# A fused two-layer recurrent block: FFN pair 1 at the end of a round, decayed keys turned through memory, and three other moves

## What is computed

```python
xn = _layernorm(x)
s  = _L0_attn_ref(xn, ...)          # recurrent attention with a decay per channel and token
g  = _silu(_L0_ffn_ref(xn, ...))    # gated FFN 256 -> 1024, 2 of 4 kept by magnitude, -> 256
x  = x + s * g
xn = _layernorm(x)
s  = _L1_attn_ref(xn, ...)          # state space layer, 8 heads, states of 64
g  = _silu(_L1_ffn_ref(xn, ...))    # gated FFN
x  = x + s * g
```

## Time and profile before

| | us |
|---|---|
| median of 3 runs (lowest to highest) | 735.85 (734.74 to 736.4) |
| the profiled execution | 735.66 |
| its span | 733.9 |
| PE busy | 711.3 (97%) |
| DVE busy | 497.5 (68%) |
| ACT busy | 342.0 (47%) |
| POOL busy | 77.2 (11%) |
| mean granted TensorE clock, 1 is full | 0.995 |
| PE's share of the chain that ended last | 76% |

### The profile page before, as it was taken

How to read it: one execution, slowest core, us unless ns; L and a number is a source line. 1 busy time by engine, 2 the same in 40 slices (tenths; PEclk the granted TensorE clock), 3 DMA queues, 4 the chain that set the end, 5 groups by cost and what they waited for, 6 DMA issues and landing times.

```text
span 733.9 us, 17949 instructions
## 1 busy us (share of the span) xinstructions
PE 711.3 (97%) x6896; PEld 590.1 (80%) x6896; DVE 497.5 (68%) x1207; ACT 342.0 (47%) x678; POOL 77.2 (11%) x85
## 2 busy tenths in 40 slices
PE   5998999999999999999999999999999999999998
PEld 3777688877888688886888868888788878888686
DVE  4976599547895478955787558855689547895133
ACT  1411685226832468215762168522584236821690
POOL 6301011101011010100111001110101101011020
PEclk9989999999999999999999999999999999999999
DMA  7900351125400353013531145102540136301360
GB/s 238 404 23 29 102 88 32 15 73 144 75 2 15 88 146 59 2 28 104 117 59 16 30 138 95 32 15 69 142 80 3 15 87 145 59 2 26 119 116 16
DMA packets 122444, 55.93 MB, mean 76 GB/s; under 512 B 104384, under 2 KB 114176, under 8 KB 120832
## 3 DMA queue, kind: packets, MB, share of 16 engines
q1 hardware_dynamic: 122368, 54.76, 30.3%
HBM read 42.35 MB, written 12.40 MB: 75 GB/s over the span
## 4 chain that ended last, share of the span: by engine, by line
PE 76%; DVE 12%; issue 5%; DMA 2%; SPq 2%; ACT 2%; POOL 1%; DVEq 0%; ACTq 0%; POOLq 0%
PE psum L1486 58%; PE psum L1707 2%; PE psum L1722 2%; PE psum L1514 2%; PE psum L1565 1%; PE psum L1760 1%; PE psum L1931 1%; PE psum L1595 1%; PE psum L1733 1%; DVE beats L1085 1%; PE psum L1577 1%; DVE own L992 1%; PE psum L1554 1%; PE psum L1873 1%; SPq L453 1%
## 5 line engine op out<-in xcount | busy, mean ns | idle before, releaser
L602 ACT ACTIVATE BC<-psum 64x256 f32<-64x256 f32 x128 | 81.4, 636 | 3.0 <-PE psum L1486 1.3
L1486 PE MATMUL psum<-xn1T,sb_n_gate 128*128 128x256 f32 x256 | 61.3, 382 | 0.0
L1486 PE MATMUL psum<-xn1T,sb_n_up 128*128 128x256 f32 x256 | 60.6, 380 | 0.4 <-DVE cs_row L1294 0.4
L1486 PE MATMUL psum<-xnT,sb_f_gate 128*128 128x256 f32 x240 | 58.5, 386 | 0.0
L1486 PE MATMUL psum<-xnT,sb_f_up 128*128 128x256 f32 x240 | 57.6, 382 | 0.0
L733 ACT ACTIVATE thFB<-psum 128x512 f32<-128x512 f32 x8 | 4.8, 597 | 104.9 <-PE psum L1486 104.9
L1486 PEld LDWEIGHTS psum<-xn1T,sb_n_up 128*128 128x128 f32 x256 | 48.0, 190 | 6.9 <-DVE cs_row L1294 0.8
L1486 PEld LDWEIGHTS psum<-xn1T,sb_n_gate 128*128 128x128 f32 x256 | 48.0, 190 | 6.8
L1486 PEld LDWEIGHTS psum<-xnT,sb_f_up 128*128 128x128 f32 x240 | 44.8, 190 | 6.4 <-issue 0.3
L1486 PEld LDWEIGHTS psum<-xnT,sb_f_gate 128*128 128x128 f32 x240 | 44.2, 189 | 6.8 <-issue 0.2
L1486 PE MATMUL psum<-sb_f_down,hid 128*128 128x256 f32 x224 | 49.5, 379 | 0.0
(11 more groups left out here) (257 smaller groups left out, 1459.0 us busy)
## 6 DMA issues: line engine op xcount, KB each, us to landing
cs_row<-cs_dram SPq DMA_DIRECT2D x8, 1024.0 KB, 4.9
x_dram<-gate SPq DMA_DIRECT2D x8, 512.0 KB, 2.8
cs_half<-cs_dram SPq DMA_DIRECT2D x16, 256.0 KB, 5.9
hidB<-x_dram SPq DMA_DIRECT2D x8, 512.0 KB, 5.9
b_dram<-B_turned SPq DMA_DIRECT2D x32, 128.0 KB, 3.3
hidB<-b_dram SPq DMA_DIRECT2D x8, 512.0 KB, 4.2
X<-in_x SPq DMA_DIRECT2D x9, 256.0 KB, 3.5
XT<-in_x_turned SPq DMA_DIRECT2D x8, 256.0 KB, 3.6
```

The costliest lines, as they stand in the source:

```text
L602: ins = a_.activation(cols[:, par, 2 * pair:2 * pair + 2, :], src[64 * par:64 * par + 64, :, s, :], ACT.Identity)
L1486: ins = t_.matmul(ps(t, name)[first_row:first_row + rows, col:col + n], w, x, start=(k == 0), stop=(k == len(ws) - 1))
```

## The change

- Pair 1 of the next tile follows pair 0 at the end of a round, also of the first one, where it takes the place of six idle matmuls; it is gone from the first third. Its two names move to banks 4 and 7, ACT makes SiLU of both gates at the end of a round (`next_gates`) with the table for exponentials behind them, and DVE needs one instruction in place of two for pair 1.
- From the second round on the keys for `kv` go another way: DVE's `keys_to_end` scales and copies them (three instructions with the transpose), SP stores eight pieces to a new `k_dram` and loads them as token rows (`key_rows`), PE's transposes and ACT's copy are gone, and `chunk_states` waits for the load. It stands behind `within`, and `across` goes ahead of `outputs`.
- `high_levels` goes behind the gate of pair 2, next to the scores. `res0` goes ahead of the gate's projection. ACT makes `end_exp` and the first `L_exps` ahead of `gate_tanh`. The three comparisons of pairs 0 and 1 stand together before the levels. POOL's mask waits until the fourth level is made.
- First round: idle matmuls have 128 columns (4 behind `p2g`, 9 in `yT`), parts of the down projection stand between the last level, `keys_turned`, `chunk_states` and `outputs`. Last round: `B0` goes ahead of `carries`.

```diff
-FILLS = [["mix_w", "dw", "w0", "k", "mix_g0", "L0", "M0", "k0T", "p3g", "F0"],
-         ["p0g", "mix_k", "w1", "p1g", "mix_g1", "L1", "M1", "kv", "p3u", "yT"],
-         ["p0u", "mix_r", "p1u", "r", "D0", "g", "p2g", "Y0", "s0"],
+FILLS = [["mix_w", "dw", "w0", "mix_g0", "L0", "M0", "p3g", "kv", "F0"],
+         ["p0g", "mix_k", "w1", "mix_g1", "L1", "M1", "p3u", "yT"],
+         ["p0u", "mix_r", "k", "r", "D0", "g", "p2g", "Y0", "s0"],
          ["a", "mix_v", "v", "D1", "p2u", "Y1"],
-         ["csum", "C1", "sc0", "st", "n0u", "n2u", "F1"],
+         ["csum", "C1", "sc0", "st", "n0u", "n2u", "F1", "p1u"],
          ["dt", "B0", "res0", "sc3", "n0g", "n2g", "s1"],
          ["X0", "B1", "res1", "sc1", "ys1", "n1u", "n3u"],
-         ["X1", "C0", "sc2", "ys0", "n1g", "n3g"]]
+         ["X1", "C0", "sc2", "ys0", "n1g", "n3g", "p1g"]]
 BANKS = len(FILLS)
...
-               ["p0g", "w0", "D0", "mix_g0", "g", "xT1"], ["p0u", "w1", "D1", "mix_g1", "F0"], ["p1g", "p2g", "yT"], ["p1u", "p2u", "s0"]]
+               ["p0g", "w0", "D0", "mix_g0", "g", "next_p1u"], ["p0u", "w1", "D1", "mix_g1", "F0"],
+               ["p1g", "p2g", "yT", "xT1"], ["p1u", "p2u", "s0", "next_p1g"]]
 FIRST = {n: (b, i + 1) for b, names in enumerate(FIRST_FILLS) for i, n in enumerate(names)}
...
...
+        return b, self.count(PER[b], NTH[name] + EXTRA[b] - behind * PER[b])
     def at(self):
...
-            return name not in ("p0", "p1", "p2") or (name == "p2" and t.first) or (name == "p0" and not t.first)
+            return name not in ("p0", "p1", "p2") or t.first == (name == "p2")
...
+            def key_rows(a):
+                wait(k_rows, a.count(16, 0))
+                wait(k_blocks, a.count(1, 0))
+                to = A["k_dram"].rearrange("(j a h i b) -> i h a j b", a=32, h=CH, i=4, b=32)
+                for i in range(4):
+                    for h in range(CH):
+                        sp_.dma_start(to[i, h], k0_turned[32 * i:32 * i + 32, h * T:(h + 1) * T].rearrange(
+                            "p (j b) -> p j b", b=32)).then_inc(k_stored, 16)
+                wait(k_stored, a.count(128, 0))
+                sp_.dma_start(k0n[:, :, :].rearrange("p a b -> p (a b)").rearrange("p (q c) -> p q c", q=NQ),
...
+                        key_rows(a)
                         token_rows(a)
...
+                    if a:
+                        pool.wait_ge(lev_ready, a.count(6, 4))
+                        pool.sem_inc(passed, 1)
                     g.affine_select(out=cs_row[:, :, :], in_=cs_row[:, :, :], compare_op=ALU.is_ge, fill=NEG, base=0,
                                     pattern=[[0, NQ * SCH], [1, P]], channel_multiplier=-1).then_inc(cs_masked, 1)
...
+                def next_gates():
+                    for n in range(2):
+                        ffn_tanh(a.next(), f"p{n}", th[n], None)
+                    exp_tables()
...
-                    ffn_tanh(a, "p0", th[0], th_ready)
-                    exp_tables()
                     rank_tanh()
...
-                    ffn_tanh(a, "p1", th[1], th_ready)
+                    ffn_abs(a, 1)
...
                     copy(a, v[:, :, :], "v", NQ)
-                    ffn_abs(a, 1)
                     receptances()
                     bc(b, "B0", 0, 0)
                     bc(b, "B1", 0, 1)
                     bc(b, "C0", 1, 0)
                     bc(b, "C1", 1, 1)
-                    gate_tanh()
                     end_exp()
                     L_exps(0)
+                    gate_tanh()
                     act.wait_ge(X_stored, b.count(16, 32))
                     res_tanhs(0)
                     res_tanhs(1)
                     others()
...
                     sums_exp()
                     ffn_tanh(a, "p3", th[1], th_ready, "p1")
...
                     rank_tanh()
                     ffn_tanh(a, "p0", th[0], th_ready)
...
                     squares()
                     out_scaled()
                     ffn_tanh_0()
+                    next_gates()
                     copy(a, xn1T[:, :, :], "xT1", CH)
                     wait_freed(act, a, "xT1")
                     act.sem_inc(xn1_loaded, 16)
...
-                k_ins, q_ins = level_update(t, 64)
-                k_ins.then_inc(k0_ready, 1)
-                q_ins.then_inc(q0_ready, 1)
+                if t.first:
+                    k_ins, q_ins = level_update(t, 64)
+                    k_ins.then_inc(k0_ready, 1)
+                    q_ins.then_inc(q0_ready, 1)
+                    return
+                two = block_decay(64).rearrange("p (b two) -> p b two", two=2)
+                qq = halves(flat(rT), 64)
+                d.tensor_tensor(qq[:, :, 1, :], qq[:, :, 1, :], two[:, :, 0:1].to_broadcast([P, CH * NQ, 64]),
+                                ALU.mult).then_inc(q0_ready, 1)
+            def keys_to_end(t):
+                dve.wait_ge(lev_ready, t.count(6, 6))
+                dve.sem_inc(passed, 1)
+                two = block_decay(64).rearrange("p (b two) -> p b two", two=2)
+                kk, to = halves(flat(kT), 64), halves(flat(k0f), 64)
+                did(d.tensor_tensor(to[:, :, 0, :], kk[:, :, 0, :], two[:, :, 1:2].to_broadcast([P, CH * NQ, 64]), ALU.mult))
+                did(d.tensor_copy(to[:, :, 1, :], kk[:, :, 1, :]))
+                after()
+                d.transpose(k0_turned, flat(k0f)).then_inc(k_blocks, 1)
             def sparse_compare(t, m, i):
...
                     hidden_p(a, 0)
+                    hidden_p(a, 1)
                     mix_scaled(a, "w")
                     mix_add(a, "w")
                     mix_scaled(a, "k")
...
                     decay_sums(a)
-                    hidden_p(a, 1)
+                    compare(0)
                     mix_g_scaled(a)
                     mix_add(a, "g")
-                    sparse_compare(a, 0, 0)
...
                     own_taken(a)
-                    end_args()
                     B_by_block(0)
                     B_by_block(1)
+                    end_args()
                     level_next(a, 4)
                     level_next(a, 5)
                     low_taken(a)
                     gate_0()
+                    keys_to_end(a)
+                    res_gate(0)
+                    res_gate(1)
                     high_taken(a)
                     last_update(a)
-                    res_gate(0)
-                    res_gate(1)
-                    sparse_compare(a, 0, 1)
-                    sparse_compare(a, 0, 2)
                     B_decayed()
                     decayed_scores(0)
+                    decayed_scores(1)
+                    hidden_p(a, 2)
+                    decayed_scores(2)
+                    decayed_scores(3)
+                    states_1()
                     states_0()
-                    for n in (2, 1, 3):
-                        decayed_scores(n)
-                    hidden_p(a, 2)
-                    states_1()
                     hidden_p(a, 3)
                     sparse_count()
                     sparse_select(0)
...
+                    sparse_compare(a, 1, 1)
                     states_0()
-                    sparse_compare(a, 1, 1)
...
-                    wait_freed(pe, a, "k0T")
+                    if a.first:
+                        wait_freed(pe, a, "k0T")
+                    else:
+                        pe.wait_ge(k_rows, a.count(16, 16))
+                    pe.sem_inc(passed, 1)
...
-                        t_.matmul(ps(a, name)[:, 0:C], ident[:, :], W["f_gate"][:, 0:C], start=True, stop=True)
+                        t_.matmul(ps(a, name)[:, 0:P], ident[:, :], W["f_gate"][:, 0:P], start=True, stop=True)
...
                     carries()
-                    project_p(a, 1, "u")
-                    project_p(a, 1, "g")
                     keys()
...
                     low_levels(a)
+                    ssd_proj(b, "res0", "w_res", 0)
                     gate_in()
-                    ssd_proj(b, "res0", "w_res", 0)
                     ssd_proj(b, "res1", "w_res", 1)
                     project_p(a, 2, "u")
+                    project_p(a, 2, "g")
                     high_levels(a)
-                    project_p(a, 2, "g")
-                    keys_turned()
                     scores(0)
                     scores(1)
-                    chunk_states()
                     project_p(a, 3, "g")
                     project_p(a, 3, "u")
                     states()
                     within()
+                    chunk_states()
+                    across()
                     outputs()
-                    across()
...
                         next_up_0()
+                        ffn_p(a.next(), 1)
...
-                    kept_at_work("p2u", 1)
+                    kept_at_work("p2u", 4)
...
                     level_last(a)
-                    keys_turned()
-                    chunk_states()
                     pe.wait_ge(loads["down0"], 16)
                     pe.wait_ge(sparse_ready, a.count(2, 1))
```

(19 more changed lines are left out.)

28 lines of the change are left out of this document (20 added, 8 removed).

## The result

The changed kernel takes **740.34 us** (median of 7 runs, 738.63 to 742.47) against 735.15 for the kernel before (7 runs): ratio 1.0075, interval 1.0059 to 1.0092. That is slower by 0.75%, clear of the interval, where the prediction said 728.6 and gave "slower" a chance of 0.09. Its profiled execution took 740.57, span 738.9.

The account below looks back on a forecast made before the run. PE, busy 97% of the span, was taken as the bound, so only savings on PE counted. Terms -3.3 - 0.7 - 0.4 - 0.3 + 1.0 - 3.4 = -7.1 took 735.66 to 728.6 us, range 723.5 to 735.0.

Parts of the forecast that it names:

- the five rivals: Clock falls 0.29; no bank 2 wait 0.10; mask delays or thin slacks 0.12; late keys 0.09; pair 1 saves nothing.
- (d): Rival: keys come late through memory, PE stands at kv, kernel slower, 740.6 for a 12 us trip; chance 0.09.
- Pair 1, -3.3: Moving pair 1 to the round's end saves 3.46 us in the seventh round and costs 0.1 in the first.
- "Nothing loses its cover": After pair 1's move, values, keys and receptances come 3.46 us earlier, yet PE meets no new wait; costed at nothing.
- POOL's mask, -0.3: Starting the mask after the fourth level removes PE's 0.34 us wait beside a DVE comparison, in the second round alone.
- Wait for bank 2, +0.8: Each round PE waits at pair 2's gate until DVE's gate_0, held by ACT's late tanh, frees the bank: +0.8 us.
- A looped round, +0.15: Transposes gone -0.53, gate wait gone -0.22, bank 2 wait +0.8, outputs' wait +0.1; +1.0 us over seven rounds.
- Keys through memory: In looped rounds the keys' store and load take 7.8 us and arrive 2.5 us before kv needs them.
- The clock, -3.4: In the first round, extra idle matmul work keeps PE's clock full between 34 and 42 us, saving 3.4 us.
- First stretches: Forecast changes by stretch: first round -3.7 us, first looped round -0.85, seventh and last rounds -3.3.

Follow-up runs that it names:

- the hint: One more PE instruction at the top of each looped round, naming the jump at its end: changed kernel 728.12 us, kernel before 732.07.
- b_slot219: Kernel before with its PE loop's first instruction placed at slot 219 of a 256-instruction block: 746.87 us, ratio 1.0163.
- a_pad204: Changed kernel with 204 additions to an unread semaphore ahead of PE's first matmul, shifting its instruction stream: 773.25 us, ratio 1.0531.
- b_hint_idle4: Kernel before with the hint and, in the first round's gap, four idle matmuls of 128 columns for one of 256, others halved: 732.18 us.
- b_pad132: Kernel before with 132 additions to an unread semaphore ahead of PE's first matmul: 751.91 us, ratio 1.0248.
- b_pair_k_pool_hint: Kernel before with the hint, pair 1 at the previous round's end, keys in bank 2 and POOL's mask waiting for the fourth level: 734.13 us, ratio 1.0008.
- slot 0: PE's loop placed with its first instruction at the start of a 256-instruction block: changed kernel 729.27 us, kernel before 731.79.
- b_pad52: Kernel before with 52 additions to an unread semaphore ahead of PE's first matmul: 746.72 us, ratio 1.0203.
- a_slot232: Changed kernel with its PE loop's first instruction placed at slot 232 of a 256-instruction block: 738.86 us, ratio 1.0084.

## Why the prediction was wrong

**The step that failed** is a term of the sum that was put at nothing without a reason: the reading of PE's instructions. Every instruction was costed at the time that it takes or waits, the looped round at +0.15, as if its instructions were always there. The 52 that PE got ahead of its loop moved the loop's place against the blocks in which instructions are read, and at the new place five looped rounds stalled behind the jump: without the hint the changed kernel takes 11 us more than with it, the kernel before 2.4. The kernel before stalls in the same way when it is put there (b_slot219), so the place does it, not the new order; but a_pad204 shows that the old place is no better for the new order. None of the five rivals had it; (d) gave nearly the right time (740.6) for another reason. With the hint the changed kernel takes 728.12, and the forecast was 728.6. That agreement is luck: the forecast started from a kernel that carried 2.4 us of fetch itself, and hint against hint only some 3 of its 7.1 us are there. The terms:

- **Pair 1, -3.3.** "Nothing loses its cover" was wrong. Alone the pair costs 7.8, and it needs two other edits, the keys' bank (priced at 0) and POOL's wait (-0.3); even with both it took 2.1 more than its partner, so no run shows the 3.3 by themselves. What stands for them is one stretch of profiles: seventh and last round together, 135.2 before and 132.9 after, both with the hint.
- **POOL's mask, -0.3.** It carries 9.8 in the new order. The forecast quoted the rule that DVE with two SBUF inputs and POOL exclude each other, but applied it to the comparison that stood beside the mask before, not to what would stand beside it after.
- **Wait for bank 2, +0.8.** Measured 0.75 (4.5 us over six rounds). The chain behind it, which the forecast read from the earlier trace rows, was half wrong: ACT's tanh ends late, but DVE is busy with the levels until 0.3 before. The changed kernel's timeline, DVE:

```profile
188.72 0.50 DVE L1027 COPY_PREDICATED own<-masks,psum 128x128 f32<-128x128 int8 x2
189.52 0.69 DVE L1208 SCALAR_TENSOR_TENSOR gT<-gT,psum 128x512 f32<-128x512 f32 x1 [0.30 <-ACT gT L714]
```

and PE:

```profile
190.26 2.00 PE L1536 MATMUL psum<-xnT,sb_f_gate 128*128 128x256 f32 x8 [0.75 <-DVE gT L1208]
```

- **A looped round, +0.15.** With the hint 87.40 against 87.38 before (rounds 2 to 6, 437.02 and 436.91 by five). But the kernel before carried fetch too: hint to hint it is 87.40 against 87.0, +0.4. So the new wait for the bank cost what the transposes saved, and a little more.
- **Keys through memory.** In time, as forecast, with less to spare than the 2.5. SP in the changed kernel:

```profile
191.58 5.35 SPq L397 DMA_DIRECT2D k_dram<-mixed_k  x8
198.23 0.38 SPq L400 DMA_DIRECT2D mixed_w<-k_dram  x1
```

and PE, which doesn't wait:

```profile
201.69 0.63 PE L1927 MATMUL psum<-v,mixed_w 128*64 128x64 f32 x16
```

  The load is issued 6.7 behind SP's first piece, not 5.1, and the last of its packets moves between 200.2 and 200.6: 1.1 us are left. Rival (d) was nearer than 0.09 made it look, though it did not come.
- **The clock, -3.4.** In the profiles with one idle matmul of 256 columns in that gap it fell in the first round in 5 of 9 (in four of them behind that gap, in b_pad132 behind PE's wait for the turned keys), in those with four of 128 in 0 of 11. That supports the step, but b_hint_idle4 shows no gain in the median (+0.1), so its size in the typical run is not shown; it mostly narrows the spread. The earlier trace rows show one execution, and I took its fall for the rule. Elsewhere the changed kernel lost clock that nobody had counted: 1.6 us behind one of its stalls.
- **First stretches.** First round -4.1 for -3.7; first looped round -1.5 with the hint (-1.3 without) for -0.85. The seventh and last gained 2.6 with the hint, not 3.3: PE's wait for `cs_row` in the last round grew from 0.4 to 0.8 (1.0 without the hint).

## To carry to other kernels

When PE's stream is long and has a loop, look at the instruction queue's packets and at "issue" gaps inside a group of matmuls before believing a difference of a per cent: compare both versions with the jump's target hinted or the loop placed, or the effect of the loop's new place is read as that of the edited work. When a step is taken out of an early stretch, everything behind it comes nearer to the loads and to the other engines' work that is tied to the round's start: list what will lie side by side in the new order and ask which pairs exclude each other. And try edits in the company that they need: the pair's move cost 7.8 us alone and 10.4 with the keys' bank, and one wait of POOL's gave 8.4 of it back.

## What the hardware showed that was not expected

- A block of 256 PE instructions came 2.8 to 3.4 us behind the round's first matmul after a jump back, 2.4 to 3.0 behind its packet. Among the small matmuls of the levels PE can use up the 256 in less: 32 of them and as many weight loads take 0.46 us in b_pair_k_pool_hint, so 256 take some 1.8 (an estimate from that).
- A hint of one instruction, or slot 0 for the loop, took the packets from 66 to 21; the kernel before gained 0.3%, the changed one 1.5%.
- An addition to a semaphore costs PE about 0.15 us: from 52 to 80, 132 and 204 of them its first matmul moves from 10.2 us to 14.5, 22.4 and 33.5. Some of the first lay in the wait for the first tile, which ends at 7.4.
- The fall of the granted clock between 34 and 42 us comes in some executions of the same order and not in others.
- A stall of PE can be followed by a fall of the granted clock to the 1.2 GHz level (0.57 of full from 429 to 433 us in the changed kernel), which cost another 1.6 us. It came behind one of the five stalls in the changed kernel and two of five in b_slot219, all three of 1.7 us, but behind none of the five in b_pad52 and in a_slot232, of 1.35 to 1.77.
